# Loading the first pair's ids directly, ahead of the scratch round trip, in a DLRM tower kernel

## The reference

```python
e = jnp.stack([tbl_0[ids[:, 0]], tbl_1[ids[:, 1]],
...
 axis=1)                                            # (2048, 32, 64)
gram = jnp.einsum('bnd,bmd->bnm', e, e)
rows, cols = jnp.triu_indices(32, k=1)
z = gram[:, rows, cols]                             # (2048, 496)
h = jnp.concatenate([z, dense_ctx], axis=1)         # (2048, 512)
h = jnp.maximum(h @ W_top1 + b_top1, 0.0)           # 512
h = jnp.maximum(h @ W_top2 + b_top2, 0.0)           # 256
y = h @ W_top3                                      # 1
```

## Time and profile before

| | |
|---|---|
| median of 3 runs | 421.31 us (420.28 to 423.41) |
| the profiled execution | 422.96 us |
| its span, first to last instruction | 421.2 us |
| TensorE busy | 383.8 us (91%) |
| VectorE busy | 229.9 us (55%) |
| POOL busy | 276.7 us (66%) |
| ScalarE busy | 166.7 us (40%) |

### The profile page before, as it was taken

One profiled execution on the slowest core, in us unless ns is written; L12 is line 12 of the kernel. 1 busy time (PEld: TensorE's weight loads), 2 busy tenths in 40 slices (PEclk: granted clock), 3 DMA queues, 4 the chain that ended last, 5 costly groups with the idle time before them and its releaser, 6 DMA issues.

```text
span 421.2 us, 15063 instructions
## 1 busy us (share of the span) xinstructions
PE 383.8 (91%) x6516; PEld 214.8 (51%) x6516; DVE 229.9 (55%) x717; ACT 166.7 (40%) x264; POOL 276.7 (66%) x746
## 2 busy tenths in 40 slices
PE   0668777998989999999999999999999999989998
PEld 0334333555545555555446554555445555554576
DVE  2899999864647886017168886017158982000000
ACT  4346666522117835221444435221354425231222
POOL 7888888864446888565588998565588888410000
PEclk9999999999989999999999999999999999998999
DMA  5944841210003786100187622100177111015610
GB/s 162 381 143 138 261 165 42 47 42 18 19 17 62 142 206 209 20 19 16 31 161 163 192 67 49 19 20 17 23 143 166 37 21 23 16 29 105 121 52 0
DMA packets 38236, 37.51 MB, mean 89 GB/s; under 512 B 13781, under 2 KB 26903, under 8 KB 38042
## 3 DMA queue, kind: packets, MB, share of 16 engines
q1 hardware_dynamic: 29546, 28.54, 26.6%
q0 software_dynamic: 6144, 6.30, 7.2%
q10 hardware_dynamic: 2480, 1.71, 1.5%
HBM read 28.45 MB, written 8.09 MB: 87 GB/s over the span
## 4 chain that ended last, share of the span: by engine, by line
PE 76%; DVE 15%; ACT 3%; DMA 3%; issue 2%; ACTq 1%; DVEq 0%
PE sel_ps L522 37%; PE tower_ps L568 13%; DVE onehot L467 11%; PE gram_ps L553 10%; PE tower_ps L578 6%; PE gat_ps L522 3%; PE gat_ps L538 3%; PE tower_ps L522 3%; DVE tabs L455 2%; DVE work L450 2%; ACT vecs L333 2%; PE tower_ps L587 1%; DMA ids_wide<-ids_scratch 1%; DMA ids_scratch<-sel_f 1%; ACTq L181 1%
## 5 line engine op out<-in xcount | busy, mean ns | idle before, releaser
L467 DVE TENSOR_SCALAR onehot<-ids_wide,row_ids 128x512 bf16<-128x512 f16 x688 | 201.3, 364 | 101.0 <-PE sel_ps L522 86.4
L296 POOL DMA_INDIRECT rows<-in_tbl_dram,gat_ids x192 | 195.8, 1020 | 74.0 <-PE gram_ps L553 55.5
L522 PE MATMUL sel_ps<-onehot,tabs 128*64 128x512 bf16 x1872 | 211.7, 382 | 30.0 <-DVE onehot L467 17.7
L522 PEld LDWEIGHTS sel_ps<-onehot,tabs 128*64 128x64 bf16 x1872 | 110.6, 110 | 126.0 <-issue 30.0
L333 ACT COPY vecs<-sel_ps 64x256 f32<-64x256 f32 x144 | 87.2, 606 | 95.4 <-PE sel_ps L522 75.8
L292 POOL MEMSET spare<- 128x1 f32 x546 | 80.7, 148 | 20.4
L568 PE MATMUL tower_ps<-work,w_sb 128*128 128x512 f32 (+1 forms) x160 | 58.7, 515 | 0.2 <-ACT h L356 0.2
L553 PEld LDWEIGHTS gram_ps<-vecs 64*32 64x32 f32 x4096 | 38.4, 105 | 25.4 <-issue 25.3
L553 PE MATMUL gram_ps<-vecs 64*32 64x32 f32 x4096 | 42.5, 201 | 4.4 <-issue 4.3
L568 PEld LDWEIGHTS tower_ps<-work,w_sb 128*128 128x128 f32 x160 | 29.2, 190 | 20.9 <-issue 18.5
L474 DVE COPY work<-gram_ps 128x512 f32<-128x512 f32 x8 | 5.2, 685 | 54.6 <-PE gram_ps L553 54.6
(11 more groups left out here) (19 smaller groups left out, 64.4 us busy)
## 6 DMA issues: line engine op xcount, KB each, us to landing
ids_wide<-ids_scratch SPq DMA_DIRECT2D x40, 256.0 KB, 6.6
rows<-in_tbl_dram,gat_ids POOLq DMA_INDIRECT x192, 2.5
products<-work SPq DMA_DIRECT2D x12, 248.0 KB
products<-work SPq DMA_DIRECT2D x24, 120.0 KB
work<-in_packed_dram SPq DMA_DIRECT2D x5, 512.0 KB, 5.7
work<-products SPq DMA_DIRECT2D x9, 256.0 KB, 4.5
work<-in_packed_dram SPq DMA_DIRECT2D x3, 640.0 KB, 5.3
work<-in_packed_dram ACTq DMA_DIRECT2D x2, 512.0 KB, 4.4
```

The lines of the kernel that those rows point to most:

```text
L296: nc.gpsimd.indirect_dma_start(out=rows[:, r, k, h, :], out_offset=None, in_=tables[GATHERED[k]], in_offset=bass.IndirectOffsetOnAxis(ap=g ...
L467: last = nc.vector.tensor_scalar(onehot[:, n % RING, c - c0, :], ids_wide[:, k, :], row_ids[chunks[k]][:, c:c + 1], None, ALU.is_equal)
L522: last[at] = nc.tensor.matmul(sel_bank(u, g)[DIM * at:DIM * at + DIM, :], tabs[:, first_chunk[k] + c, part, :], onehot[:, piece_no(u, g, h ...
```

## The change

A new input, `ids_first`, holds the int32 ids of unit 0 and pair 0 alone. SP loads it to all partitions into a part of `h1`, which is not in use by then, right behind the first gathered ids (512 KB). VectorE casts it into `ids_wide`. SP also loads table 1 there, behind the ids and ahead of its wait for the cast of `sel_ids`; before, ScalarE issued that load. The wide load of pair 0 in unit 0 goes, and the other wide loads and tables keep their order. VectorE's order of unit 0 becomes: cast, half 0 of pair 0, rest(0), piece 2, low(0), piece 3, rest(1), half 0 of pair 1, low(1), rest(2), half 1 of pair 1, low(2), rest(3), and from pair 2 on as before.

```diff
--- before.py
+++ after.py
@@ -74,7 +74,7 @@
     return n * (2 * FIELDS - 1 - n) // 2 + m - n - 1
 
 
-def dlrm_tower_kernel(nc, chunks, ctx_t, ids_gat, ids_sel, tables, packed, w1, b1, w2, b2, w3, out):
+def dlrm_tower_kernel(nc, chunks, ctx_t, ids_gat, ids_first, ids_sel, tables, packed, w1, b1, w2, b2, w3, out):
     first_chunk = [sum(chunks[:k]) for k in range(N_SEL)]
     halves = [((0, c // 2), (c // 2, c)) for c in chunks]
     half_most = max(b - a for h in halves for a, b in h)
@@ -114,6 +114,8 @@
         b1_sb = sb("b1_sb", [P, J1], F32)
         b2_sb = sb("b2_sb", [P, J2], F32)
         h1 = sb("h1", [P, J1, UNIT], F32)
+
+        first_ids = h1[:, 0:WIDE, :].bitcast(I32)
         h2 = sb("h2", [P, J2, UNIT], F32)
         spare = sb("spare", [P, 1], F32)
         y = [sb(f"y{b}", [1, UNIT], F32) for b in range(2)]
@@ -128,7 +130,9 @@
                     for u in range(UNITS)]
 
         gat_ids_in = [sem(f"gat_ids_in{i}") for i in range(2)]
+        first_ids_in = sem("first_ids_in")
         sel_ids_in = sem("sel_ids_in")
+        first_ids_cast = sem("first_ids_cast")
         sel_f16_ready = sem("sel_f16_ready")
         scratch_out = sem("scratch_out")
         wide_in = [sem(f"wide_in{w}") for w in range(N_SEL // WIDE)]
@@ -231,16 +235,18 @@
 
             first = ROUNDS * 2 * N_GAT
             sp.dma_start(gat_ids[:, 0:first], ids_gat[:, 0:first]).then_inc(gat_ids_in[0], 16)
+            sp.dma_start(first_ids, ids_first.partition_broadcast(P)).then_inc(first_ids_in, 16)
+            load_stage(1)
             sp.wait_ge(sel_f16_ready, 1)
             sp.dma_start(ids_scratch.rearrange("u k x -> (u k x)").rearrange("(p x) -> p x", p=P), sel_f16[:])\
               .then_inc(scratch_out, 16)
             sp.wait_ge(scratch_out, 16)
-            load_wide(0, 0)
+            load_wide(0, 1)
             load_stage(2)
-            load_wide(0, 1)
+            load_wide(0, 2)
             load_stage(3)
             sp.dma_start(gat_ids[:, first:], ids_gat[:, first:]).then_inc(gat_ids_in[1], 16)
-            for w in range(2, N_SEL // WIDE):
+            for w in range(3, N_SEL // WIDE):
                 load_wide(0, w)
             for g in range(STAGE_SLOTS, N_PAIRS):
                 load_stage(g)
@@ -371,10 +377,7 @@
                 nc.scalar.copy(y[v % 2][:, 0:width], tower_ps[0:1, v % 2, 0:width]).then_inc(y_ready, 1)
 
             act.dma_start(sel_ids[:], ids_sel).then_inc(sel_ids_in, 16)
-            for g in range(2):
-                act.dma_start(stage[g][:, 0:pair_chunks[g][1], :],
-                              packed[:, pair_chunks[g][0]:pair_chunks[g][0] + pair_chunks[g][1], :])\
-                   .then_inc(stage_in[g], 16)
+            act.dma_start(stage[0][:, 0:pair_chunks[0][1], :], packed[:, 0:pair_chunks[0][1], :]).then_inc(stage_in[0], 16)
             high(0)
             middle(0)
             high(1)
@@ -441,7 +444,10 @@
         def _(dve):
             dve.wait_ge(sel_ids_in, 16)
             nc.vector.tensor_copy(sel_f16[:], sel_ids[:]).then_inc(sel_f16_ready, 1)
+            dve.wait_ge(first_ids_in, 16)
+            nc.vector.tensor_copy(ids_wide[:, 0:WIDE, :], first_ids).then_inc(first_ids_cast, 1)
             dve.wait_ge(row_ids_ready, len(row_ids))
+            dve.wait_ge(first_ids_cast, 1)
 
             def rest(g):
                 dve.wait_ge(hi_ready, g + 1)
@@ -455,10 +461,10 @@
                 nc.vector.tensor_tensor(tabs[:, c0:c0 + k, 2, :], stage[g % STAGE_SLOTS][:, 0:k, :],
                                         tabs[:, c0:c0 + k, 1, :], ALU.subtract).then_inc(tabs_ready, 1)
 
-            def one_hots(u, g, half):
-                if half == 0:
-                    dve.wait_ge(wide_in[g], 16 * (u + 1))
-                for at in range(2):
+            def one_hots(u, g, half, fields=(0, 1)):
+                if half == 0 and (u, g) != (0, 0):
+                    dve.wait_ge(wide_in[g], 16 * (u if g == 0 else u + 1))
+                for at in fields:
                     k, n = 2 * g + at, piece_no(u, g, half, at)
                     if n >= RING:
                         dve.wait_ge(onehot_used, n - RING + 1)
@@ -474,14 +480,19 @@
                     nc.vector.tensor_copy(gram_rows[:, r, h, :, 16 * b:16 * b + 16],
                                           gram_ps[:, h, :, :].rearrange("p i m -> p m i")).then_inc(gram_emptied, 1)
 
+            one_hots(0, 0, 0)
             rest(0)
+            one_hots(0, 0, 1, (0,))
             low(0)
-            one_hots(0, 0, 0)
+            one_hots(0, 0, 1, (1,))
             rest(1)
-            one_hots(0, 0, 1)
+            one_hots(0, 1, 0)
             low(1)
             rest(2)
-            for g in range(1, N_PAIRS):
+            one_hots(0, 1, 1)
+            low(2)
+            rest(3)
+            for g in range(2, N_PAIRS):
                 one_hots(0, g, 0)
                 if g + 1 < N_PAIRS:
                     low(g + 1)
@@ -689,6 +700,7 @@
     laid = {
         "ctx_t": given["dense_ctx"].T,
         "ids_gat": ids[..., GATHERED].transpose(3, 4, 0, 2, 1, 5).reshape(P, -1),
+        "ids_first": ids[0][..., SELECTED[0:WIDE]].transpose(4, 0, 1, 2, 3).reshape(WIDE, UNIT),
         "ids_sel": ids[..., SELECTED].transpose(0, 5, 1, 2, 3, 4).reshape(P, -1),
         **{f"tbl_{f}": given[f"tbl_{f}"] for f in GATHERED},
         "packed": packed,
```

More of the change, by code:

```diff
@@ L717 @@
     chunks = [inputs[f"tbl_{f}"].shape[0] // KROWS for f in SELECTED]
-    dlrm_tower_kernel(nc, chunks, args["ctx_t"], args["ids_gat"], args["ids_sel"], tables, args["packed"], args["w1"],
-                      args["b1"], args["w2"], args["b2"], args["w3"], out)
+    dlrm_tower_kernel(nc, chunks, args["ctx_t"], args["ids_gat"], args["ids_first"], args["ids_sel"], tables,
+                      args["packed"], args["w1"], args["b1"], args["w2"], args["b2"], args["w3"], out)
     r = _run(nc, [arrays], core_ids=[0])
```

## The result

| | before | after |
|---|---|---|
| median of 17 runs each | 421.94 us | 425.39 us |
| lowest to highest | 419.73 to 423.71 | 423.07 to 428.05 |
| ratio, 95% interval | | 1.0082 [1.0061, 1.0104] |
| the profiled execution | 422.96 us | 423.29 us |
| its span | 421.2 us | 421.5 us |

The change makes the kernel 3.5 us slower. It was forecast 0.3 us faster, with 2.2 us slower as the end of the range. The profiled execution of the changed kernel is among its quickest (423.29 of 423.07 to 428.05), so its span says less than the stretches within it. (The mean granted clock is TensorE's over a whole execution, on record in steps of 0.004. It counts stretches at a lower clock and doesn't say where they lie.)

A forecast was written before the change was run, and what follows sets the result against it. VectorE's work at the start of unit 0 was taken to set the pace, then TensorE. Gain 6.0 - A, with A = 5.7, is 0.3 us: median 421.31 to 421.0, range 418.0 to 423.5.

The forecast's parts named there:

- the milestone: Start of one_hots(0, 2, 0) on VectorE, 26.39 before; forecast at A + 20.4, near 26.1.
- The sign: Whole kernel: the forecast is wrong if the milestone and the span do not move together.
- A: Time when the first pair's ids have landed on all partitions; taken as 5.7 us, the middle, with 4.9 to 6.6.
- The upper bound of 6.6: Ids' landing if they end after table 0: 1.24 MB moved by 6.0 us, plus 0.6; loss 0.6 us.
- The 8.2 of the slow first load: Far bound of A at the first wide load's 116 GB/s: loss 2.2 us; rival 2 beyond 6.6, chance 0.20.
- My estimate by it, 6.0: Ids' landing by the skill page: 1.24 MB at 1.2 + 2.0 + 2.8 us, putting the gain at nothing.
- The ring wait: VectorE before one_hots(0, 1, 0): piece 4 waits for TensorE's half 0 of pair 0, 2.3 us idle.
- rival 1: TensorE's first half takes 2.78 us, stall 0.9: gain 1.7 us with A = 5.7; chance 0.15 for 1.3 to 3.3.
- The cast: Added on VectorE, first ids, 128x1024: taken as 1.1 us, bounds 0.33 and 1.21.
- The moved loads: Table 1, scratch, pair 1's wide ids and table 2 stay hidden; the last two covered by 3.9 and 2.6 us.
- The hand-over: At 69.66 and 73.43 VectorE's lateness passes through ScalarE to TensorE's pair 8; a microsecond there is one of the kernel.
- The sum: Gain to the milestone is 6.0 - A; with A = 5.7, 0.3 us gained.

The follow-up runs named there:

- all_four: Changed kernel with pair 0's copies ahead of middle(3), own buffers for pieces 4 and 5, 42 added matmuls, table 0 behind the ids: 422.94 us, ratio 0.9994.
- copy_ahead: Changed kernel with ScalarE's copies of pair 0 moved ahead of middle(3): 422.99 us, ratio 1.0020 to the kernel before.
- late_piece: Changed kernel with low(2) placed between the two pieces of half 1 of pair 1: 422.69 us, ratio 1.0034 to the kernel before.
- table_ahead_of_ids: Changed kernel with pair 0's copies ahead of middle(3), and table 1 issued ahead of the ids instead of behind: 423.91 us, ratio 1.0060 to the kernel before.
- ids_first: Changed kernel with table 0 issued by SP behind the ids instead of by ScalarE beside them: 425.17 us, ratio 1.0035 to the kernel before.
- before_copy_ahead: Kernel before, with ScalarE's copies of pair 0 moved ahead of middle(3): 422.01 us, ratio 0.9994 to the kernel before.
- own_buffers: Changed kernel with buffers of their own for pieces 4 and 5: 422.94 us, ratio 1.0019 to the kernel before.
- warm_start: Changed kernel with 42 matmuls of the identity added ahead of pair 0 on TensorE: 424.64 us, ratio 1.0024 to the kernel before.
- before_long_gap: Kernel before, with the cast high(4) ahead of the copies of pair 0 on ScalarE: 424.01 us, ratio 1.0055.

## Why the prediction was wrong

**What failed.** The step was: "After it [the milestone] the program of every engine is the same in both kernels, so whatever the change wins or loses at that point goes through to the end." The program is the same, the distances between engines are not. Before, rest(3) came straight behind the last piece of pair 1; now low(2) stands between them, and TensorE ends pair 1 sooner (27.72 against 25.39 + 2.78 = 28.17) while rest(3) starts later (25.95 against 25.26). Its idle time grew by 1.1 us to 2.9, it restarted at half clock, and the ring passed that on to VectorE, which sets the pace. I had put the order of the last pieces of pair 1 down as work that only adds up. The sign I had named for it was there: the milestone came 0.7 us late, pair 8 2.0 us and the median 3.5. The step doesn't hold for a gain either, as all_four shows. Price, from copy_ahead: 2.6 us. From late_piece, which moves one piece and so shortens the idle time: 2.0. Both are differences between sets. In the one trace VectorE waited 1.2 us for it, and TensorE's half took 1.6 longer.

**A, mis-sized.** Forecast 5.7, with 4.9 to 6.6; it was 6.71, and 6.62 to 6.88 in every kernel that loaded the ids in this place beside table 0. The middle of two bounds was the choice that cost: the ids took 5.0 to 5.7 us from issue to the cast, with table 0 beside them or not. The upper bound of 6.6, both transfers ending last, came nearest, though not for its reason alone: without table 0 beside them the cast still came at 6.24. The 8.2 of the slow first load was farther off than the 5.7. The Trainium skill's fit of a fixed part of 2.0 us and bytes at 436 GB/s (DMA: Bandwidth & Descriptors, section "Anatomy of one DMA") is given there for transfers issued by GpSimd. My estimate by it, 6.0, was nearer than my middle and still 0.7 early for this load, which SP issues.

**The ring wait, right in kind and short in size.** It was forecast at 2.3 us and was 2.28 in the profile of the changed kernel. That it fits so well is luck of one execution: the same wait is 2.58 us in late_piece, 3.03 in table_ahead_of_ids, 3.14 in copy_ahead and 3.17 in ids_first. For the first half varies: from TensorE's start to VectorE's one-hots of pair 1 it took 4.5 us in the changed kernel's profile, 5.4 in copy_ahead, 5.3 in table_ahead_of_ids, 5.4 in ids_first and 4.9 in late_piece, against 4.3 of my sum, so on average 0.8 more. In the kernel before this is covered: 1.2 us of slack, and in before_copy_ahead, where the slow weight loads go on until 19.4, VectorE's one-hots of pair 1 start at 19.40 without a wait. I had given a chance to a shorter first half (rival 1) and none to a longer one. The Trainium skill says that the number of slow matmuls at a kernel's start varies from run to run (TensorE: Matmul & The Clock Gate, section "What's actually happening"). The traces agree: 14 in the kernel before, 28 in own_buffers.

**The cast** was 0.3 us cheaper than taken, 0.81 from start to start in place of 1.1. **The moved loads** were hidden, as forecast. **The hand-over** at pair 8 is as described: what VectorE lost there TensorE lost.

**The sum again,** with what was measured: 6.0 - 6.7 + 0.3 for the cast - 0.8 for the slow half is a loss of 1.2 us, which is what copy_ahead shows (1.0020, 0.8 us, with an interval up to 2.0). With 2.6 for pair 2 it makes 3.8, beside the 3.5 measured; but the 2.6 is itself the changed kernel less copy_ahead, so that this checks only the 1.2. With the 1.2 us that VectorE waited in the trace in its place the sum is 2.4, short of the measured interval (2.6 to 4.4 us).

**What stays open.** Why the first transfers take five microseconds even when little shares the engines; why the half clock comes in some executions and not in others at the same idle time; what the rest of the price of pair 2 is, beyond the 1.2 to 1.6 us of the trace; and why a lead at pair 8 shrank in all_four.

## What to carry to other kernels

When an order is changed, add up not only each engine's work to a milestone but also the idle time of the others on either side of it: an idle stretch that was harmless can become long enough for TensorE to restart at half clock, and a short ring hands that to the engine that sets the pace. Slack that hides a start-up cost belongs in the sum as a stock that the change may spend; here 1.2 us of it covered a slow first half whose length, in other executions, was up to 0.9 us above what one profile showed. And where a program's time varies by a per cent from run to run, compare the executions with the same mean granted clock with each other, beside all of them: the first shows what the edit costs at full clock, the count of the others how often the clock fell. Where it fell only a trace can say.

## What the runs showed of the hardware

Idle times of TensorE of up to 1.95 us ahead of pair 2 were followed by full pace in every profile of this study; after 2.73 to 2.93 us the clock was 0.50 in three profiles (the changed kernel, own_buffers and ids_first, 9.7 to 9.9 us for 72 matmuls) and full in two (warm_start, before_long_gap). The length alone doesn't settle it: with 2.9 us in the trace, 0 of 17 executions of the changed kernel had a mean clock of 1.000 and 7 of 12 of own_buffers. Slow matmuls at the start of the first pair numbered 14 to 28 in the profiles without added matmuls, while the windows over them show a granted clock of 1.00. With 42 matmuls added ahead of pair 0, executions at a mean clock of 1.000 fell from 20 of 35 to 1 of 12 in the kernel before; the lower clock of its profile lies between 370 and 390 us. A load of 512 KB to all partitions and one of 256 KB, each right behind the 24 KB of gathered ids on SP, released their casts within 0.3 us of each other (6.62 to 6.85 and 6.88).
